# A dense block ahead of the sorted expert tiles, a third activation buffer, and low halves moved from GpSimd to VectorE, in a graph-attention and mixture-of-experts kernel

## The reference

```
h = inlayer2 @ W.T + b;  f1 = h @ w1 + b1;  f2 = h @ w2 + b2
coefs = softmax(leaky_relu(f1[:, None] + f2[None, :]) where adj > 0, else -1e9)
x = x + coefs @ layernorm(x)
n = layernorm(x)
probs = softmax(n @ gate_w + gate_b);  cw = probs at its two largest, 0 elsewhere
x = x + sum over e of cw[:, e] * (gelu(n @ W1[e] + b1[e]) @ W2[e] + b2[e])
```

## Time and profile before

| | |
|---|---|
| median of 3 runs | 515.39 us (514.81 to 516.31) |
| profiled execution, its own time | 514.22 us |
| its span, first to last instruction | 512.0 us |
| TensorE busy | 424.5 us (83%) |
| VectorE busy | 375.0 us (73%) |
| GpSimd busy | 229.0 us (45%) |
| ScalarE busy | 182.5 us (36%) |
| mean granted TensorE clock | 0.963 of 2.4 GHz |

### The profile page before, as it was taken

The page is one execution under the profiler, slowest core; times in us unless marked ns, Lnnn a source line. Parts: engine busy times, 40 slices in busy tenths (PEclk is TensorE's granted clock), DMA queues, the critical chain, the costliest instruction groups (busy, mean ns, idle before and its releaser), DMA issues.

```text
span 512.0 us, 6657 instructions
## 1 busy us (share of the span) xinstructions
PE 424.5 (83%) x2198; PEld 227.1 (44%) x2198; DVE 375.0 (73%) x792; ACT 182.5 (36%) x315; POOL 229.0 (45%) x262
## 2 busy tenths in 40 slices
PE   3799999999899799999999998004698998888884
PEld 3682434345234244453444443003466764555553
DVE  0437679898999998989999995001677976566656
ACT  1529910123210210202212021003767765666562
POOL 8902302011029520121000577671476778759990
PEclk9999999999999999999999999555989999999999
DMA  6999999999719999398000011114133311181002
GB/s 190 182 106 105 105 106 216 160 152 92 73 12 102 193 173 105 29 84 81 1 1 0 1 48 48 48 53 143 33 94 92 98 58 37 37 225 37 28 22 63
DMA packets 45398, 43.96 MB, mean 86 GB/s; under 512 B 4419, under 2 KB 41555, under 8 KB 45109
## 3 DMA queue, kind: packets, MB, share of 16 engines
q0 software_dynamic: 20928, 25.13, 41.0%
q1 hardware_dynamic: 23684, 18.39, 13.0%
q10 hardware_dynamic: 752, 0.02, 0.1%
HBM read 81.86 MB, written 11.99 MB: 183 GB/s over the span
## 4 chain that ended last, share of the span: by engine, by line
DVE 33%; PE 31%; ACT 12%; POOL 9%; DMA 8%; issue 7%; ACTq 0%; SPq 0%; DVEq 0%; POOLq 0%
DVE c L999 15%; PE bank L1219 15%; POOL sorted_x L509 9%; DVE maskT L1072 6%; ACT maskT L710 4%; DMA x<-in_x 4%; DVE maskT L767 4%; ACT g_row L703 3%; PE bank L1135 3%; DMA share<-in_L_gnn_inlayer 3%; PE bank L1283 2%; PE bank L1254 2%; DVE xs L841 2%; ACT share L591 1%; PE bank L1267 1%
## 5 line engine op out<-in xcount | busy, mean ns | idle before, releaser
L1219 PE MATMUL bank<-c,Y 128*128 128x512 f32 x512 | 236.1, 604 | 14.1 <-DVE c L999 13.2
L999 DVE SCALAR_TENSOR_TENSOR c<-g_row,r_col,maskT 128x512 f32<-128x512 f32 x256 | 189.5, 781 | 13.3 <-PE bank L1219 10.7
L1219 PEld LDWEIGHTS bank<-c,Y 128*128 128x128 f32 x512 | 90.8, 189 | 142.9 <-DVE c L999 83.7
L523 POOL DMA_INDIRECT choice_y<-Y,mask x54 | 62.9, 1164 | 24.2 <-issue 14.9
L504 POOL TENSOR_TENSOR rows<-xn,rows 128x512 f16<-128x512 f32 x6 | 8.8, 1468 | 121.4 <-ACT rows L634 121.4
L509 POOL DMA_INDIRECT sorted_x<-rows,share x40 | 47.7, 1192 | 23.4 <-DVE share L970 11.6
L1072 DVE SCALAR_TENSOR_TENSOR maskT<-g_row,maskT 128x1024 f16<-128x1024 f32 x24 | 31.1, 1296 | 31.3 <-ACT maskT L710 31.3
L1254 PE MATMUL bank<-ident,mask 128*128 128x128 f16 x108 | 11.1, 228 | 38.8 <-DMA mask<-sorted_x 33.6
L703 ACT ACTIVATE g_row<-bank,b1T 128x512 f32<-128x512 f32 x48 | 30.5, 684 | 33.3 <-DVE maskT L1072 31.4
L437 POOL DMA_DIRECT2D mask<-in_adj x24 | 15.8, 665 | 57.8 <-DVE maskT L767 57.6
L767 DVE STREAM_TRANSPOSE maskT<-mask 128x1024 uint32<-128x1024 uint32 x32 | 39.5, 1236 | 0.0
(11 more groups left out here) (195 smaller groups left out, 687.1 us busy)
## 6 DMA issues: line engine op xcount, KB each, us to landing
mask<-in_adj POOLq DMA_DIRECT2D x24, 512.0 KB, 17.6
mask<-in_adj POOLq DMA_DIRECT2D x32, 128.0 KB, 26.2
mask<-sorted_x SPq DMA_DIRECT2D x27, 132.0 KB, 2.2
sorted_x<-share SPq DMA_DIRECT2D x2, 1584.0 KB, 11.3
maskT<-choice_y SPq DMA_DIRECT2D x10, 256.0 KB, 4.8
share<-in_L_gnn_inlayer SPq DMA_DIRECT2D x2, 1024.0 KB, 10.2
share<-in_x POOLq DMA_DIRECT2D x8, 256.0 KB, 12.4
out<-x SPq DMA_DIRECT2D x8, 256.0 KB, 2.3
```

The source lines that it names most:

```text
L523: pool.indirect_dma_start(out=choice_y, out_offset=bass.IndirectOffsetOnAxis(ap=xt_id[:, t % XR, i, D:D + 1].bitcast(U32), axis=0), in_=y_ ...
L999: dve.scalar_tensor_tensor(c[:, k % CR].rearrange("p (s i) -> p s i", i=32), g_row[:, s * ST:s * ST + ST].rearrange("p (s i) -> p s i", i= ...
L1219: mm(bank[:, par, :], Y[:, k], c[:, k % CR], start=(k == 0), stop=(k == NK - 1)).then_inc(c_used, 1)
```

## The change

- The list ITEMS sets a new order: the eight dense steps of supertile 5, then the 27 tiles, then the 16 dense steps of supertiles 6 and 7. All engines walk through it; banks go by the place in it. What supertile 7 owes stands in the first nine items.
- `hd` has GR = 3 buffers.
- Routing has three groups: the sorted blocks, supertile 5, and supertiles 6 and 7. The first is done wholly in supertile 6, with a step before and after c, and rank after k = 11; the second in supertile 7; the third from item 12 on.
- The shares of the two choices are written into spare words of `rows`, travel with the rows into the tiles, and `evict` multiplies by them, as two scalings of 128 columns. `ffn2` adds the low product onto the high one in the bank and begins with the bias. GpSimd no longer weighs; between the two rounds of placements it copies the second shares.
- `low_rows` is gone: `post_c` on VectorE makes the low half for every supertile at k = 23.
- `split_b2` is gone: ScalarE makes the high half, VectorE the low half on one partition in supertile 2 at k = 26, and a small transfer moves it.
- SP stores supertile 5 after the load of tile 12.

The diff, cut to its core:

```diff
+    GR = 3
     HEAD = 5
-    GROUP = ((0, HEAD * TS), (HEAD * TS, NK))
+    GROUP = ((0, HEAD * TS), (HEAD * TS, HEAD * TS + TS), (HEAD * TS + TS, NK))
...
+    ITEMS = [("dense", j) for j in range(E)] + [("tile", t) for t in range(NT)] + [("dense", j) for j in range(E, ND)]
+    FIRST = E
...
-        hd = g_row[:, 0:2 * FC * ST].rearrange("p (r f t) -> p r f t", r=2, f=FC)
+        hd = g_row[:, 0:GR * FC * ST].rearrange("p (r f t) -> p r f t", r=GR, f=FC)
...
-        share = gr[:, 2496:2560].rearrange("p (v n) -> p v n", v=2)
+        share = rows[:, 0:HEAD * TS, D + 1:D + 3].rearrange("p n v -> p v n")
...
-        b2_raw = gr[0:2, 3072:3072 + E * D]
+        b2_raw = gr[0:1, 3072:3072 + E * D]
+        b2_low = share3[0:1, YR * TP * RW:YR * TP * RW + E * D // 2].bitcast(F16)
...
+        TX = 5
         YB = (6, 1)
-        HD = ((2, 3), (4, 5))
-        STD, LOGIT, EXP = 2, 7, 9
+        HD = ((2, 3), (4, 0))
+        CHOOSE = 12
...
-            for i in range(2):
-                sp.dma_start(b2_raw[i:i + 1], b2.rearrange("(a e) d -> a (e d)", a=1)).then_inc(b2_in, 16)
+            sp.dma_start(b2_raw, b2.rearrange("(a e) d -> a (e d)", a=1)).then_inc(b2_in, 16)
+            sp.wait_ge(b2_lo, 1)
+            sp.dma_start(b2hl[1:2], b2_low).then_inc(b2_split, 16)
...
+                if t == XR:
+                    store_dense(HEAD)
...
-            store_dense(HEAD)
...
-            def split_b2():
...
-            def low_rows(s):
...
                 pool.wait_ge(sorted_in[0], 16 * n1)
-                pool.tensor_scalar(row_id[:, 0:n1], row_id[:, 0:n1], float(N), None, ALU.add).then_inc(ids_moved, 1)
+                pool.tensor_scalar(row_id[:, 0:n1], row_id[:, 0:n1], float(N), None, ALU.add)
+                pool.tensor_copy(share[:, 0], share[:, 1]).then_inc(ids_moved, 1)
                 pool.wait_ge(ids_moved, 1)
...
             for s in range(4, NS):
-                low_rows(s - 4)
                 load_adj(s, s % 2)
                 if s == 5:
-                    split_b2()
                     pool.wait_ge(wsplit, 2)
                     pool.memset(fill, 0.0).then_inc(pool_step, 1)
                     pool.wait_ge(pool_step, 11)
                     pool.iota(fill[:, :, D].bitcast(I32), [[P, YR * TP]], base=2 * N, channel_multiplier=1).then_inc(fill_made, 1)
-            low_rows(4)
-            low_rows(5)
...
                 pool.wait_ge(yin_in[s], 32)
-                for v in range(2):
-                    for i in range(TS):
-                        ins = pool.tensor_scalar(yin[:, s, v, i], yin[:, s, v, i], share[:, v, s * TS + i:s * TS + i + 1], None,
-                                                 ALU.mult)
-                ins.then_inc(weighed, 1)
-                pool.wait_ge(weighed, s + 1)
                 pool.tensor_tensor(yin[:, s, 0], yin[:, s, 0], yin[:, s, 1], ALU.add).then_inc(first_added, 1)
...
-                need(act, xld_ready, s - HEAD - 1)
+                need(act, xld_ready, s)
...
+                if s == HEAD:
+                    act.wait_ge(b2_split, 16)
...
-                    if p == 0 and s == HEAD + 1:
-                        route_exp(0)
+                    if p == 0 and s > HEAD:
...
+                        act.wait_ge(b2_in, 16)
+                        act.activation(b2hl[0:1], b2_raw, ACT.Copy, scale=W_SCALE).then_inc(b2_hi, 1)
...
-                    need(act, dlow_done, j - 1)
-                    act.activation(hd[:, j % 2, f], bank[:, HD[j % 2][f], :], ACT.Gelu,
-                                   bias=b1T[:, FC * STEPS_D[j][1] + f:FC * STEPS_D[j][1] + f + 1],
-                                   scale=1.0 / (X_SCALE * W_SCALE)).then_inc(dgelu_done, 1)
+                    need(act, dlow_done, j + 1 - GR)
+                    act.activation(hd[:, j % GR, f], bank[:, HD[ITEMS.index(("dense", j)) % 2][f], :], ACT.Gelu,
+                                   bias=b1T[:, FC * e + f:FC * e + f + 1], scale=1.0 / (X_SCALE * W_SCALE)).then_inc(dgelu_done, 1)
...
+            for i, (kind, m) in enumerate(ITEMS):
+                if i + 1 < len(ITEMS) and ITEMS[i + 1] == ("tile", 0):
+                    act.wait_ge(expert_ready, 1)
+                if i + 1 < len(ITEMS) and ITEMS[i + 1][0] == "tile":
+                    copy_x(ITEMS[i + 1][1])
+                if kind == "tile":
+                    experts.append(act.value_load(expert[0:1, m:m + 1], min_val=0, max_val=E - 1))
+                    gelu(m)
+                else:
+                    gelu_dense(m)
+                if i > 0 and ITEMS[i - 1][0] == "dense":
+                    high_dense(ITEMS[i - 1][1])
...
+                if i == CHOOSE:
+                    route_exp(2)
...
                         dve.wait_ge(post_step, (s - 1) * POST + (1 if k == BN[1] else 2))
+                    if s == HEAD + 1 and (4 <= k < 10 or k >= 13):
+                        next(routers[0], None)
                     dve.scalar_tensor_tensor(
...
-                    if last and k == 23:
+                    if not first and k == 23:
                         post_c(s - 1)
...
-                    if s == HEAD + 1 and k == 1:
+                    if s == 2 and k == 26:
+                        dve.wait_ge(b2_hi, 1)
+                        dve.wait_ge(wsplit, 2)
+                        dve.scalar_tensor_tensor(b2_low, b2_raw, W_SCALE, b2hl[0:1], ALU.mult, ALU.subtract).then_inc(b2_lo, 1)
+                    if s == HEAD + 1 and k == 0:
                         route_a(0)
-                    if s == HEAD + 1 and (6 <= k < 19 or k >= 23) or last:
+                    if s == HEAD + 1 and (3 <= k < 10 or k >= 13):
                         next(routers[0], None)
+                    if last and k == 0:
+                        route_a(1)
+                    if last and k >= 5:
+                        next(routers[1], None)
...
             def evict(t):
-                both = bank[:, YB[t % 2], :].rearrange("p (s v d) -> p s d v", s=TP, v=2)
                 dve.wait_ge(ffn2_done, t + 1)
                 need(dve, y_out[t % YR], 16 * TP * (t // YR))
-                dve.tensor_reduce(y_sb[:, t % YR], both, AX_X, ALU.add).then_inc(y_done, 1)
+                for i in range(TP):
+                    ins = dve.tensor_scalar(y_sb[:, t % YR, i], bank[:, YB[(FIRST + t) % 2], D * i:D * i + D],
+                                            xt[:, t % XR, i, D + 1:D + 2], None, ALU.mult)
+                ins.then_inc(y_done, 1)
 
...
                 need(dve, dadded, j)
+                if j % E == 0:
+                    dve.wait_ge(cw_ready, 1 if j == 0 else 2)
+                    dve.wait_ge(x2_kept, s + 1)
...
+            def finish(item):
+                if item[0] == "tile":
+                    evict(item[1])
+                else:
+                    add_dense(item[1])
+
+            post_0(NS - 1)
+            for i, (kind, m) in enumerate(ITEMS):
+                if i == 1:
+                    post_a(NS - 1)
+                    post_sum(NS - 1)
+                    post_b(NS - 1, 0)
+                if i > 0 and ITEMS[i - 1][0] == "dense":
+                    low_dense(ITEMS[i - 1][1])
+                if i == 1:
+                    dve.wait_ge(post_step, (NS - 1) * POST + 1)
+                    post_b(NS - 1, 1)
+                if kind == "tile":
+                    high(m)
+                if i >= LAG:
+                    finish(ITEMS[i - LAG])
+                if kind == "tile":
+                    low(m)
+                if i == 3:
                     post_b(NS - 1, 2)
                     dve.wait_ge(post_step, (NS - 1) * POST + 2)
                     post_b(NS - 1, 3)
-                if t == STD + 2:
+                if i == 4:
                     post_c(NS - 1)
-                if t == LOGIT + 1:
+                if i == 8:
                     post_d(NS - 1)
-                if t == EXP:
-                    route_a(1)
...
+                if i == CHOOSE:
+                    route_a(2)
+                if i > CHOOSE:
+                    next(routers[2], None)
             low_dense(ND - 1)
-            for j in range(ND - LAG, ND):
-                add_dense(j)
+            for item in ITEMS[-LAG:]:
+                finish(item)
...
                         post_c(s - 1)
-                    if s == HEAD + 1 and k == 20:
+                    if s == HEAD + 1 and k == 11:
                         rank()
...
-            def ffn2(t):
+            def ffn2(i, t):
                 e, r = experts[t], t % HR
-                dst = bank[:, YB[t % 2], :].rearrange("p (s v d) -> p s (v d)", s=TP, v=2)
-                if t == 1:
-                    pe.wait_ge(oT_copied, NS)
-                need(pe, y_done, t - 1)
+                dst = bank[:, YB[i % 2], 0:TP * D]
+                if i >= 2:
+                    added(ITEMS[i - 2])
                 pe.wait_ge(hl_done, t + 1)
+                mm(dst.rearrange("p (s d) -> p s d", d=D), scale16[:],
```

(50 more changed lines are left out.)

148 lines of the change are left out of this document (49 added, 99 removed).

## The result

The changed kernel takes 475.42 us (474.09 to 476.35, 4 runs) against 515.10 (513.95 to 516.31, 4 runs) before: ratio 0.9227, 95% interval 0.9196 to 0.9259. The forecast was 471, range 461 to 486: right in sign and range, 4.4 us too low. The profiled execution has 474.09 for a span of 472.1, where the forecast had 469.8 for 467.6. The 4.5 us are looked for stage by stage.

The account below looks back on a forecast made before the run. Taken as bounds: VectorE in parts of the attention, GpSimd's placements before the tiles, GELU's buffer wait in dense steps. Attention end 317.5, block 33.5, 25th eviction 408.2, rest 59.4: span 467.6, time 471 us, range 461 to 486.

Parts of the forecast that it names:

- The gap without matmuls: Between attention and first sorted tile: placements start at about 273, tile at hand near 338, so placements cost nothing.
- Attention: All supertiles: terms sum to -0.4 us, ending at 317.5 instead of 317.9, bounds 314 and 323; supertile 6 gets +2.
- First block: Eight dense steps before the tiles: 33.5 us with the last supertile's work, then 8.5 to the first eviction.
- The rival that the block stumbles: First dense block: gaps bring TensorE's clock down; wholly at the lower level 49 instead of 33.5 us, time 486; chance 0.10.
- One sign that the prediction named for being wrong: First dense block: long waits of ScalarE would show the forecast wrong; no size given.
- Dense steps: With a third activation buffer a dense step takes 3.12 us instead of 3.56, bounds 2.95 and 3.56.
- The ring: Dense steps: GELU, high half, low half on ScalarE and VectorE; GELU waits for a buffer; 0.61 of 3.56 us is waiting.
- the second half of a tile has the same columns in another order: nothing: Sorted tiles: TensorE's reordered second half costs no time, with the settled pace at 1.88 us per tile.
- The eviction, which the prediction worried about: Sorted tiles: two VectorE scalings taken as equal to one reduction of 0.68 us; upper bound +2.5 us over some 8 tiles.
- only shorten work beside the path: GpSimd's weighings, 5.69 us of eight in one supertile, leave without shortening the path.
- The rival that GpSimd sets the end: End of kernel: choice placements, loads and adds on GpSimd finish last, 474 us, 479 with slower adds; chance 0.10.
- The rest: After the 25th eviction: 59.4 us instead of 94.5, as eight dense steps go and 15 shorten by 0.44.

## Why the prediction was right, point by point

- **The gap without matmuls is filled.** Right: placements forecast near 273, seen at 271.73; first tile at hand before TensorE wants it. With the old order 16 us of wait are back.
- **Attention.** Forecast to end at 317.5, seen at 318.10, by errors that cancel. Supertile 2 +1.7 (forecast +1.9), 3 -4.1 (-4.05), 4 and 5 -0.3 each (-0.25), 7 +0.2 (+0.5), all near; 1 is +0.3 (-0.25). With the low rows back on GpSimd supertile 3 takes 31.86, so 3.8 of its 4.1 are `split_b2`'s, as forecast. Supertile 6 is +4.1 where the step said +2 with bounds 0 and +5: the steps squeezed in two by two stall TensorE, and the clock falls behind the stall; undone, 3.65 come back. Against it stand 1.5 us at the start (supertile 0 ends at 82.99 instead of 84.53), which the change doesn't touch: over the kernels run here that end moved between 82.1 and 84.9.
- **First block.** Forecast from the attention's end to the first eviction 42.0, seen 42.6. The rival that the block stumbles was right in kind and small in size: a mean clock of 0.95 from 318.10 to 351.00, which is the lower level for some 3 us of the block (an estimate from that mean), not for all of it. The Trainium skill, "TensorE: Matmul & The Clock Gate", section "What's actually happening", has the array throttled unless activity releases it; the trace agrees for a wait of 3.96 inside a block that is otherwise dense. One sign that the prediction named for being wrong did come, long waits of ScalarE in the block: 2.67 us for the row factors, and 3.7 behind it for TensorE.
- **Dense steps.** Forecast 3.12; seen 3.10 (two steps from 431.46 to 437.65), and 3.44 for the last ones, beside GpSimd's adds. The ring was the limit, as two buffers show.
- **The failed step is "the second half of a tile has the same columns in another order: nothing".** It costs 0.30 us a tile against the pace of before, 0.23 against the same kernel with the old second half and eviction (1.95). Where the pace is settled, from tile 8 to 19, that is 3.3 us, most of the 4.0 between tiles 0 and 24 and of the whole miss. What the columns left out is a gap of 0.28 us at TensorE's read of the expert number and 0.19 beside the bias, 0.47 a tile against 0.23 before; why the read costs more behind the new second half stays open. The eviction, which the prediction worried about, was equal: two scalings of 0.34 on VectorE, 0.60 from start to end as they overlap, and the profile shows no wait of TensorE for them in the settled tiles.
- **GpSimd.** The prediction said that its weighings leave and "only shorten work beside the path". That holds against the long path of before; against the path of after it does not: with the weighings GpSimd sets the end, and the kernel takes 497.10 us. The rival that GpSimd sets the end, which counted no weighings, did not come: the last add ends at 462.4, 9.7 us ahead of the span's end.
- **The rest** from tile 24: forecast 59.4, seen 472.1 - 413.42 = 58.7.

## What to carry to other kernels

Equal columns were not equal time here, in a stage of short products that reads a register for each tile: look at TensorE's gaps in the trace before costing a reordering at nothing. Before an idle gap is filled with other work, cost again everything that the gap had hidden, GpSimd's transfers and end work above all. Two gains that end at the same wait don't add: here an earlier attention and a shorter block both run into the 60 us of placements.

## What was not expected of the hardware

- The granted clock near 0.5 came behind waits of TensorE, but not behind each. Waits of 3.96 and 3.98 in the block were followed by 0.69 and 0.50, and 0.59 and 0.56, one of 4.16 by 0.50, one of 1.65 in supertile 6 by 0.62 and 0.52. A wait of 1.69 at 325.15 in the kernel after was followed by 1.00; the same wait at 325.14, with the row factors early, by 0.62 and 0.53. By these two windows up to 1.7 us (an estimate: 0.38 and 0.47 of 2 us each) may come and go with an edit that stands later in the block than the wait.
- Twelve more TensorE instructions per tile were free, while the gap at the one register read was 0.14 us a tile before, 0.28 after, and 0.43 where the read was moved (0.54 less the product's 0.11; 0.09 of it stood there without the read).
- `low_dense`, with both inputs in SBUF, takes 1.93 beside GpSimd's adds and 1.23 alone; `add_dense`, with one input from a bank, takes 1.11 and 1.12. The Trainium skill, "SBUF — State Buffer", section "Who interferes with whom", says that a VectorE instruction with two SBUF inputs contends with a GpSimd instruction that reads SBUF; the trace agrees.
- The first placement took 7.69 us before and 1.34 to 2.84 in the kernels here; what made it long was not tried.
